# A transformer layer with adaptive conditioning, one core: the condition's silu as the first step, and the start's steps and loads in another order

## The reference

```python
cond = jax.nn.silu(c) @ wc.T + bc
sh1, sc1, g1, sh2, sc2, g2 = jnp.split(cond, 6, axis=-1)
...
h = _ln(x) * (1.0 + sc1) + sh1
x = x + g1 * _gqa_attn(h, wq, wk, wv, wo)
h = _ln(x) * (1.0 + sc2) + sh2
x = x + g2 * _mlp(h, w1, b1, w2, b2)
```

## Time and profile before

| | us |
|---|---|
| median of 3 runs | 1416.48 (1416.14 to 1418.04) |
| the profiled execution | 1418.17 |
| its span in the trace | 1416.2 |
| from the span's start to the first score (L1267) | 70.72 |

### The profile page before, as it was taken

How to read it: one execution, slowest core, us unless ns; L and a number is a source line. 1 busy time by engine, 2 the same in 40 slices (tenths; PEclk the granted TensorE clock), 3 DMA queues, 4 the chain that set the end, 5 groups by cost and what they waited for, 6 DMA issues and landing times.

```text
span 1416.2 us, 19196 instructions
## 1 busy us (share of the span) xinstructions
PE 1381.6 (98%) x6681; PEld 991.2 (70%) x6681; DVE 881.1 (62%) x1481; ACT 763.5 (54%) x1375; POOL 641.7 (45%) x279
## 2 busy tenths in 40 slices
PE   6999999999999999999999999899999999999998
PEld 4655565665656566565567878788888888888886
DVE  3687787686777768677665565755475355733243
ACT  6377758576675856667756556534443344422221
POOL 3067687685867768587810085412032010311012
PEclk9999999999999999999999999999999999999999
DMA  8332222423233242323259685476662865546523
GB/s 285 88 90 59 67 92 82 123 78 106 57 91 96 83 117 80 110 57 87 78 165 266 137 277 152 156 253 193 179 193 66 303 189 164 155 156 195 149 82 119
DMA packets 163438, 193.85 MB, mean 137 GB/s; under 512 B 59960, under 2 KB 84552, under 8 KB 163344
## 3 DMA queue, kind: packets, MB, share of 16 engines
q1 hardware_dynamic: 163344, 192.64, 45.3%
HBM read 108.91 MB, written 40.93 MB: 106 GB/s over the span
## 4 chain that ended last, share of the span: by engine, by line
PE 82%; DVE 6%; SPq 3%; DMA 3%; ACT 2%; POOL 2%; issue 1%; DVEq 0%; ACTq 0%; POOLq 0%
PE acc L2388 18%; PE proj_bank L1183 13%; PE turn L2375 9%; PE key_bank L1267 8%; PE pv_bank L1276 7%; PE row_bank L1254 7%; PE up L2375 7%; PE up L1645 4%; PE acc L2339 3%; DVE neg_max L994 2%; PE sum_bank L1286 2%; SPq L559 2%; DMA gate_now<-gate_scratch 1%; POOL probs_sum L689 1%; PE proj_bank L1193 1%
## 5 line engine op out<-in xcount | busy, mean ns | idle before, releaser
L994 DVE TENSOR_REDUCE neg_max<-row_bank 128x1 f32<-128x512 f32 x512 | 337.7, 684 | 139.1 <-PE row_bank L1254 135.2
L818 ACT ACTIVATE probs<-key_bank 128x512 f32<-128x512 f32 x512 | 299.7, 598 | 159.4 <-PE key_bank L1267 149.0
L689 POOL TENSOR_TENSOR probs_sum<-probs_sum,probs 128x2048 f32<-128x2048 f32 x62 | 285.6, 4607 | 14.1 <-ACT probs L818 7.3
L2388 PE MATMUL acc<-w_t,hidden 128*128 128x512 f32 x1152 | 269.4, 390 | 0.3 <-DVE hidden L2231 0.3
L2388 PEld LDWEIGHTS acc<-w_t,hidden 128*128 128x128 f32 x1152 | 215.8, 188 | 46.7 <-DVE hidden L2231 1.7
L1267 PE MATMUL key_bank<-q_stack,k_stack 128*128 128x512 f32 x512 | 217.4, 428 | 3.3 <-ACT probs L818 2.8
L1254 PE MATMUL row_bank<-k_stack,q_stack 96*128 96x512 f32 x512 | 203.3, 408 | 4.4 <-DVE neg_max L994 2.9
L689 POOL TENSOR_TENSOR probs_sum<-probs 128x2048 f32<-128x2048 f32 x31 | 142.6, 4600 | 81.7 <-ACT probs L818 81.7
L1839 POOL TENSOR_TENSOR y<-y,resid 128x512 f32<-128x512 f32 x30 | 41.4, 1416 | 264.9 <-DVE y L2152 264.9
L1267 PEld LDWEIGHTS key_bank<-q_stack,k_stack 128*128 128x128 f32 x512 | 96.1, 188 | 83.3 <-issue 46.9
L1254 PEld LDWEIGHTS row_bank<-k_stack,q_stack 96*128 96x128 f32 x512 | 96.3, 188 | 38.9 <-DVE neg_max L994 17.1
(11 more groups left out here) (219 smaller groups left out, 1890.1 us busy)
## 6 DMA issues: line engine op xcount, KB each, us to landing
ring<-w1s_scratch SPq DMA_DIRECT2D x168, 256.0 KB, 3.7
q_stack<-spare SPq DMA_DIRECT2D x384, 64.0 KB, 2.0
hid_scratch<-spare SPq DMA_DIRECT2D x36, 256.0 KB, 4.9
spare<-hid_scratch SPq DMA_DIRECT2D x36, 256.0 KB, 2.7
xa<-in_x_dram SPq DMA_DIRECT2D x8, 1024.0 KB, 10.0
resid<-in_x_dram SPq DMA_DIRECT2D x8, 1024.0 KB, 7.2
x_scratch<-resid SPq DMA_DIRECT2D x8, 1024.0 KB, 4.5
spare<-in_L_cond_w_dram SPq DMA_DIRECT2D x32, 256.0 KB, 3.3
```

The lines of the kernel that those rows point to most:

```text
L689: nc.gpsimd.tensor_tensor(probs_sum[:, :, :], first_in[:, :, :], probs[kt][:, :, :], ALU.add).then_inc(added, 1)
L818: nc.scalar.activation(probs[kt][:, r, :], key_bank[r % 2][:, :], ACT.Exp).then_inc(exp_done, 1)
L994: nc.vector.tensor_reduce(out=neg_max[:, g % 2, i:i + 1], in_=row_bank[(g + i) % 2][:, :], op=ALU.max, axis=AX.X, negate=True).then_inc(ro ...
L2388: last = nc.tensor.matmul(acc[tt][:, :], hidden[n % 2][i][:, tt * P:tt * P + P], w_t[:, j, 2 + k, :], start=(own == 0 and m == 0), stop=(o ...
```

## The change

Two lists change, and no instruction's work does.

```diff
 FRONT = """
-Wc0.0 Wc0.1 S Mc0.1 Wc0.2 Wc0.3 Mc0.3 Wc1.0 Wc1.1 Wc1.2 B0 X0 Mc1.1 Wc1.3 Wk.0 Wq.1 Wq.3 Wq.0 Mc1.3 B1 N0 C0 Wq.2 Wc2.0
-C1 Wc2.1 T0 Wo.1 Wc2.2 Wc2.3 T1 Mc2.1 Wo.2 T2 Wv.0 Mc2.3 T3 Wc3.0 Ka Kb Kc B2 Kd Q0a Wc3.1 Wc3.2 Q0b Wo.0 Q0c Q0d Wc3.3
-Wo.3 Mc3.1 Mc3.3 Q1a B3 r0 r1 Wc4.0 Wc4.1 C3 r2 Wc4.2 Q1b r3 r4 Mc4.1 r5 Wc4.3 r6 Wc5.0 r7 Q1c r8 Mc4.3 r9 r10 B4 Q1d Va
-r11 r12 Vb Wc5.1 Wc5.2 C4 Wc5.3 r13 Vc r14 Vd b1 r15 Mc5.1 t s0 Mc5.3 s1 Q2a s2 Q2b B5 s3 Q2c s4 Q2d
+S Wc0.0 Wc0.1 Wc0.2 B0 Wc0.3 Mc0.1 Mc0.3 Wc1.0 Wc1.1 Wc1.2 Wc1.3 X0 C0 Mc1.1 Wk.0 Wq.2 Wq.3 B1 Wq.1 N0 Mc1.3 Wc2.0
+Wc2.1 C1 Wc2.2 T0 Mc2.1 Wo.2 T1 Wq.0 Wc2.3 T2 Wo.1 Wv.0 T3 Mc2.3 Wc3.0 Wc3.1 Ka Kb Wc3.2 Kc Q0a B2 Kd Q0b Q0c Q0d
+Wc3.3 Wo.0 Wo.3 Mc3.1 Mc3.3 Wc4.0 Wc4.1 Q1a B3 Q1b r0 r1 C3 Mc4.1 r2 Wc4.2 r3 r4 Wc4.3 r5 Wc5.0 r6 r7 Q1c r8 r9 Mc4.3
+Va B4 r10 Q1d Wc5.1 r11 Vb r12 C4 Wc5.2 r13 Wc5.3 r14 Vc r15 Vd Mc5.1 t s0 Mc5.3 b1 s1 Q2a s2 B5 Q2b s3 Q2c s4 Q2d
 """.split()
...
-LOADS = ('c1', 'q', 'x', 'k', 'c2', 'o', 'v', 'c4', 'c3', 'c5', 'b3', 'b4', 'b1')
+LOADS = ('c1', 'x', 'k', 'q', 'c2', 'v', 'o', 'b3', 'b1', 'c3', 'b4', 'c5', 'c4')
```

## The result

The changed kernel takes 1408.82 us (median of five runs, 1408.32 to 1409.94), the kernel before beside it 1417.86 (median of five, 1416.14 to 1418.85). The ratio is 0.9946, 95% interval 0.9935 to 0.9957: 0.54% faster, 7.7 us at the ratio. The forecast was 1409.0, within 1406.5 to 1413.5. It was a median before of 1416.48 less 7.5 us. Beside each other the medians are 9.0 us apart, and the ratio says 7.7, so the 0.2 us between forecast and median is in part luck. The profiled execution took 1409.94 us with a span of 1407.9; the forecast for it was 1410.7.

What follows compares the result with a forecast made beforehand. The chain runs on PE for 82% of the span, and only the front before the first score can move. Terms -6.5, -1.3 and +0.3 give -7.5 us, so 1416.48 becomes 1409.0 us, range 1406.5 to 1413.5.

Steps and rivals of the forecast that it cites:

- if the stretch behind the first score changed by over 1 us: Sign that the forecast would be wrong; everything behind the first score was expected to stay at 1345.5 us.
- Step 1: Kernel start: silu moved first saves a table load and waits; bias 0 starts at 12.3, not 17.68, -5.4 us.
- Step 2: x loaded ahead of q lands at 12.7; the norm ends at 22.05 instead of 27.61, -5.55 us so far.
- Step 3: From norm's end to T3's high part: ACT's weights and T's take 10.0 us, T3 done at 31.9; clock fall +0.8.
- Step 4: From K's last quarter and Q0 to the first row scores: PE, not the stacking, sets r0 at 41.7, -6.5 us.
- the clock's 0.8: Allowance between norm and T3: PE's clock falling to half speed, costing 1.6 us, counted as half likely.
- Step 5: From r0 to the first score: two units and a quarter leave the stretch, 21.2 us instead of 22.55, -1.3 us.
- The other moves: c3, c5 and c4 held on SP until C0 and C1: cost nothing; 0.3 us put for PE's wait at C0 and the like.
- The sum: Whole front: -6.5 to r0, -1.3 in the row stretch, +0.3 for small waits, giving -7.5 us.
- VectorE did not take over the row stretch: Rival, r0 to r15: DVE's maxima replace PE as the bound, gain -5.4 or less, 1411 to 1413.7 us; chance 0.13.
- The gain was not spent on bias 1: Rival: waits at bias 1 on DVE hold the norm and T's, leaving 1414 to 1418 us; chance 0.09.
- The clock did not stay down: Rival: PE runs at 1.2 GHz from 9.4 to K's last quarter, +5.7 us, 1422.2 us; chance 0.05.

Runs made afterwards that it cites:

- the change once more: The changed kernel itself, unedited, measured again against the kernel before: ratio 0.9948, median 1409.24 us, first score at 62.22.
- the old row stretch: Changed kernel with the steps from Q1's first quarter on in the old order: ratio 0.9965 against the kernel before, first score at 63.12.
- the moved copies: Changed kernel with copies of Wc2.0, Wc2.1, Wc2.2 on VectorE and Mc2.1 behind T1: ratio 0.9940 against the kernel before, 1408.49 us, first score 61.61.
- the moved quarters: Changed kernel with three copies on VectorE, plus Q1c and Q1d earlier among the row scores: ratio 0.9949 against the kernel before, first score 62.97.
- the run with the clock kept up: Kernel before with 14 more identity transposes on TensorE ahead of C1: ratio 0.9995 against the kernel before, first score at 69.31.
- the run with TensorE at work from the start: Changed kernel with 14 identity transposes ahead of silu's: ratio 0.9953 against the kernel before, first score at 62.17.

## Why the prediction was right

**What bounds, and the remainder.** The first score was the moment to forecast, and the experiments move it and nothing else that shows. The sign "if the stretch behind the first score changed by over 1 us" was too tight: the stretch varies by 3 us between traces in which its work is the same.

**Step 1, silu first: the sign and the place right, the size not.** -5.4 with bounds -4.5 and -6.4; measured -7.11 (17.68 to 10.57), outside the bounds. The size that failed is "from 7.45 to 9.4, and the two `Mc` steps. With both at the slow rate they end at 13.2, with both at the fast rate at 11.3". The fast bound had all four units slow. In fact the second half of `wc`'s first part landed near 7.0, and TensorE's rate rose among the third and fourth units, which took 1.70 and ended at 8.7. But this is one execution. Four others with the same start (the change once more, the old row stretch, the moved copies and the moved quarters) have bias 0 at 10.98, 12.31, 11.99 and 11.53. So the date depends on when the rate rises, and three of the five lie within the forecast's 11.3 to 13.2. The landing of `c` at 2.4 was earlier than the 3.4 taken. The error hardly reached the end, because the next step has a floor of its own (the run with 12.31 was 0.14 later at `T3`).

**Step 2, x and the norm.** Forecast: x lands at 12.7 with bias 0 done at 13.7, the follow-up at 16.5, norm's end at 22.05. Measured: x at 12.9, now the later of the two (bias 0 ends at 11.96), the follow-up at 15.84, norm's end at 21.60. The landing priced from the bytes ahead was right to 0.2 us. I had written that q would cost under 0.5. It holds TensorE 1.98 us, but it costs the chain little, since the four high parts wait for the statistics until 15.84 too.

**Step 3, T0 to T3.** Forecast 10.0 us on ScalarE, to 31.9; measured 9.20, to 30.80, against 9.87 before. The term that failed is the clock's, "half of 3.2, 1.6 us", of which I took 0.8. The fall did not come, and the run with the clock kept up priced it at 0.5. ScalarE's sum was too long as well: with the clock up the stretch takes 9.20 here and 9.21 in that run, so the 10.0, borne out by the 9.87 of a stretch with the fall in it, left no room for a further price of the fall, and the 0.8 counted it twice. The mistake was to price TensorE's rate in a stretch in which ScalarE is busy 2.81 of 3.20 us.

**Step 4, K and Q0 to r0.** Forecast 41.7 with the clock's 0.8, measured 41.10; without that term 40.9. That TensorE and not the stacking would set r0 was right, and the run with the old row stretch shows both sides of it. But the near hit is two errors that cancel. `T3` was done 1.1 us early (30.80 against 31.9), and from there to r0 it took 10.30 and not 9.0. The forecast had K's last quarter start as soon as `T3`'s low part is done. That ended at 31.53, and the quarter started at 32.80, because TensorE still had a unit, a quarter of K and one of Q0 ahead of it. The three terms given for TensorE's own work up to `T3` add to 9.5 and not to the 10.0 stated, and even that was too little.

**Step 5, the row stretch.** Forecast 21.2, measured 21.29. Its 1.3 us moved, and did not vanish: of them 0.7 is gain, since r0 would have been 0.5 earlier without them.

**The other moves.** `c3` was issued at 13.89 and landed 11.6 later, at 25.5 instead of 24.8; it was wanted at 28.64. No wait for c3, c4 or c5 stands in the profile.

**The sum** was -7.5 and came out at -8.33 in the trace. The 0.8 held for the clock is as large as the difference, but the agreement of the rest is in part luck. Without it r0 comes out at 40.9, against 41.10 measured, although step 1 alone was 1.7 short in this execution: the landing of x, and TensorE's own work ahead of K's last quarter, took that back.

**The rivals.** VectorE did not take over the row stretch as a whole, only 2.7 us of it. The gain was not spent on bias 1: TensorE turned its columns at 20.27. The clock did not stay down: the granted clock is 1.00 throughout the front. The Trainium skill (TensorE: Matmul & The Clock Gate, PE-mode transpose) says the full clock does not engage for transposes; the two rows of 1.94 and 1.70 above speak against it, since the rate rose there while only transposes ran. So does the run with TensorE at work from the start, in which nothing but transposes stands ahead of the first product: there the last eight take 1.10.

How the 8.33 us divide depends on the order in which the parts are made. Silu alone gives 3.47, silu with the loads 3.62, and the remaining order the other 4.7. Taken from the other end, silu's place is worth 2.35, the loads 2.1 and the row stretch 0.7. That the parts do not add up is the result: each removes one of several waits that end close together.

## What to carry to other kernels

Behind a wait that is removed, write down the date of every transfer and engine that ends shortly after it, and let the latest of them cap the gain. A step that pays nothing alone (the loads, 0.1 us) may pay 2 us once the wait in front of it is gone, so it should be tried again then. And price TensorE's clock only where TensorE, and not the engine that empties its banks, sets the pace.

## What was not expected of the hardware

The granted clock fell in the kernel before after TensorE had stood from 25.70 to 27.28. In the changed kernel it stood longer, and the clock stayed up behind it, as its busy times show:

```profile
14.30:16.25 1.95, 0.01 (x1) 0.00 (x0) 1.66 (x7) 0.41 (x2) 0.12 (x1) 1.00 1.05 388
16.25:20.00 3.75, 3.50 (x24) 2.25 (x24) 3.05 (x5) 3.27 (x7) 1.11 (x2) 1.00 1.05 395
```

So the length of a stand alone does not tell whether the clock falls; what else does stays open here. The fall is there in the four kernels with the old order of steps and without added transposes (before, silu first, the new loads, and both), and in none with the new order.

The rise of TensorE's rate at the start also varies: bias 0 of the kernel before began at 17.68 in one execution and at 16.79 in the one with the added transposes, which came later, and the same start of the changed kernel gave 10.57 to 12.31 in five executions. The granted clock is 1.00 in the rows of that time too, while eight transposes take 1.94, so it does not show this slower rate; that it is the lower clock is not shown.

One issue on SP took 3.96 us, where its neighbours take 0.4 to 0.6:

```profile
6.23 3.96 SPq L569 DMA_DIRECT2D spare<-in_L_cond_wv_dram  x1
```

It is the eighth transfer of 256 KB or more in SP's list, and two of them had been issued under 1.1 us before. It is no accident of one execution: in all nine traces with the new loads it takes 2.9 to 4.0 us and ends at 9.8 to 10.4. `o` was thereby issued at 10.23 and landed 12.2 us later, at 22.4. In the kernel with the moved copies it landed at 22.16, and TensorE waited for it. Why this issue takes so long stays open.
